# Attention: the blocks of v loaded straight from memory on two queues, in place of a spread on GpSimd

## The chip, the cores and the metric

The kernel runs on one core of one Trainium2 chip. A core has TensorE (matrix multiply, PE in the profile, with its weight loads as PEld), VectorE (DVE), ScalarE (ACT), GpSimd (POOL) and SyncE (SP), and 16 DMA engines that move data between device memory and the on-chip memories. The metric is the device time of one execution, in microseconds (us), and the median of several executions is what counts. All data is 32-bit floating point.

## The reference, cut to what matters

The network has two parts: a gated convolution through a Fourier transform, and an attention over heads. The change is in the second alone. For every one of 8 x 56 x 56 tokens (25088 in all) it has 8 heads of 16 values.

```python
q, k, v = xs @ Wq.T, xs @ Wk.T, 2 * (xs @ Wv.T)         # each to (b, n, HEADS, DIM_HEAD)
q, k, v_h = _l2norm(q), _l2norm(k), _l2norm(v)
attn_head = softmax(einsum('bnhd,bngd->bnhg', v_h, v_h))  # 8 x 8 for each token
q = einsum('bnhg,bngd->bnhd', attn_head, q)
k = einsum('bnhg,bngd->bnhd', attn_head, k)
attn = softmax(einsum('bnhd,bnhe->bnde', k, q))           # 16 x 16 for each token
out = einsum('bnhd,bnde->bnhe', v, attn)
```

The output is then projected, and the residual is added.

## The kernel before

`build` runs its stages one after the other: weights, input projection, taps of the filter, convolution, output projection, `attend`, `project_heads`. Only `attend` changes.

`attend` works in 112 units of 224 tokens (NU), two units to a block of 448 tokens (NB = 56 blocks). A unit has 14 groups (GU) of 16 tokens. Each engine has its own program with the order written out by hand, and semaphores tie the programs together.

A block goes through a first half: TensorE projects it to q, k and v (`project`, L1180), ScalarE squares and copies (`copy_in`) and takes roots (`root`), VectorE normalizes (`normalize_q`, `normalize_kv`; the normalized v is `st_v`, L1360), GpSimd copies the norms (`copy_norm`, L1146), and ScalarE's queue stores v and the q/k rows to device memory (`store_heads`, L1283 and L1284). It is read back in another layout, one partition for each pair of token and head or of token and value. This first half runs 8 units ahead (AU) of the second.

The second half goes unit by unit. On TensorE a round i consists of `scores(i)`, `logits(i-1)`, `project(i+8)`, `mix(i)` and `outputs(i-1)`. Both `scores` (v times v, L1190) and `outputs` (L1226) read the tile `v_blocks`: 128 partitions by 14 groups by 2 rows by 64 columns, in which partition 64a + q + 4d holds value d of the token of slot (a, q), in the 8 columns of that slot, and zeros in the other 56. There are three such tiles in a ring (RING = 3).

Before the change these tiles are made in two steps. SyncE loads a block's v densely (`load_v`, L1113: 8 transfers for each block, each to every fourth of 64 partitions, four ring tiles `v_dense`); then GpSimd multiplies each dense tile, broadcast over 8 slots, by a mask `slot_of_8` (`spread_v`, L1154, once for each unit, 128 x 1792 elements). `spread_v(u)` waits until `outputs` of unit u-3 is done. After `spread_v(i+1)` GpSimd goes on to `spread_k(i)` (L1139), which makes `k_blocks` for `logits(i)` from what ScalarE's `leave_mix(i)` (L1304, L1305) wrote.

VectorE's round i is `mask(i)` (L1367, makes `e_blocks` for `mix(i)`), `divide(i-1)` (L1384 to L1390, makes `p_norm` for `outputs(i-1)`), `weigh(i)`, one half of a block's normalizing (`normalize_q` where i is even, `normalize_kv` where it is odd), `leave(i-1)` (L1395, frees the q/k rows) and `squares`. ScalarE's is `exp_s(i)`, on even i `store_heads`, then `exp_l(i-1)` (L1296), `copy_in`, `leave_mix(i)`, on even i `root` (L1277), and `copy_in` again.

The functions that the diff touches, and what calls them:

Of the kernel before, what the change touches and what calls it, by code (L numbers as in the profile page):

```python
# [13 lines left out]
HEADS, HD = 8, 16  # L14
# [53 lines left out]
def load_weights(nc, t, k):  # L68


    with ExitStack() as ctx:
# [25 lines left out]
                     (k.fwd_w[:], t.c_fwd_w), (k.tap_p[:], t.c_tap_p), (k.tap_q[:], t.c_tap_q),  # L97
                     (k.inv_w[:], t.c_inv_w), (k.dc[:], t.c_dc), (k.inv_h[:], t.c_inv_h), (k.same4[:], t.c_same4), (k.same8[:], t.c_same8), (k.slot8[:], t.c_slot8),
                     (k.rpe_in[0:2, :], t.L0_conv_rpe_in_w.rearrange("o i -> i o")),
# [926 lines left out]
def attend(nc, t, k):  # L1026
# [17 lines left out]
    RING = 3  # L1044
    NV = 4
    LOOPED = (NU - AU) // RING
    MC = (GU + 3) * HD
    MW = GU // 2 * QKM
    with ExitStack() as ctx:
# [14 lines left out]
        vb = [sb(f"v_blocks{m}", [128, GU, 2, 64]) for m in range(RING)]  # L1064
        vd = [sb(f"v_dense{m}", [128, 4 * GU, HEADS]) for m in range(NV)]
        qk = [sb(f"qk_rows{m}", [128, GU + 1, QKW]) for m in range(RING)]
# [13 lines left out]
        st_stored = [sem(f"st_stored{m}") for m in range(2)]  # L1080
        v_loaded = [sem(f"v_dense_loaded{m}") for m in range(NV)]
        qk_loaded = [sem(f"qk_loaded{m}") for m in range(RING)]
        cleared, vb_r, k_r, qkv_ps, qkv_read = sem("cleared"), sem("v_blocks_ready"), sem("k_blocks_ready"), sem("qkv_ps"), sem("qkv_read")
        nsq_r, nsc_r, nrm_r, rn_r, st_r, vn_r = (sem(n) for n in ("nsq_ready", "nsq_clamped", "nrm_ready", "rnorm_ready", "st_ready", "v_norm_ready"))
# [6 lines left out]
        def unit(i):  # L1091
            return not isinstance(i, int) or 0 <= i < NU

        @block.sync
        def _(sp):
            def load_xn(w):
                if w >= NU:
                    return
                if w >= RING:
                    sp.wait_ge(qkv_ps, 2 * (w - RING) + 2)  # L1100
                b, c = w // UPI, w % UPI
                sp.dma_start(xn[w % RING][:], t.XN[b, :, c * UT:(c + 1) * UT]).then_inc(xn_loaded[w % RING], 16)

            def load_v(n):
                if n >= NB:
                    return
                if n >= NV:
                    sp.wait_ge(vb_r, 2 * (n - NV) + 2)
                sp.wait_ge(st_stored[n % 2], 32 * (n // 2 + 1))
                v = t.VT[n * 2 * UT:(n + 1) * 2 * UT].rearrange("(x a q) (d h) -> a q d x h", q=4, a=2, h=HEADS)  # L1110
                for a in range(2):
                    for q in range(4):
                        sp.dma_start(vd[n % NV][64 * a + q:64 * a + 64:4], v[a, q]).then_inc(v_loaded[n % NV], 16)  # L1113

            def load_qk(u):
                m, n = u % RING, u // 2
                if u < RING:
                    sp.wait_ge(cleared, 1)
                else:
                    sp.wait_ge(o_r, u - RING + 1)  # L1120
                sp.wait_ge(st_stored[n % 2], 32 * (n // 2 + 1))
                sp.dma_start(qk[m][:, 0:GU, :], t.QK[u * UT:(u + 1) * UT].rearrange("(g n) h x -> (n h) g x", n=16)).then_inc(qk_loaded[m], 16)

            for w in range(AU + 1):
                load_xn(w)
            load_v(0)
            for u in range(NU):
                load_qk(u)
                load_xn(u + AU + 1)
                if u % 2 == 0:  # L1130
                    load_v(u // 2 + 1)

        @block.gpsimd
        def _(pool):
            def spread_k(i):
                pool.wait_ge(km_r, i + 1)
                if i:
                    pool.wait_ge(l_ps, i)
                pool.tensor_tensor(kb[:], bcast(km[i % 2][:], 3, 4), bcast(bcast(k.same4[:], 1, HD), 1, GU), ALU.mult).then_inc(k_r, 1)  # L1139

            def copy_norm(n):
                a = n % 2
                pool.wait_ge(nrm_r, n + 1)
                if n >= 2:
                    pool.wait_ge(st_stored[a], 32 * (n // 2))
                pool.tensor_copy(st_qk[a][:, :, :, QKM], nrm[a][:, :, 16:24]).then_inc(vn_r, 1)  # L1146

            def spread_v(u):
                n, g0 = u // 2, u % 2 * 2 * GU
                if u % 2 == 0:  # L1150
                    pool.wait_ge(v_loaded[n % NV], 128 * (n // NV + 1))
                if u >= RING:
                    pool.wait_ge(o_ps, u - RING + 1)
                pool.tensor_tensor(vb[u % RING][:].rearrange("p g r (m h) -> p (g r) m h", h=HEADS),  # L1154
                                   bcast(vd[n % NV][:, g0:g0 + 2 * GU], 2, 8),
                                   bcast(k.slot8[:].rearrange("p (m h) -> p m h", h=HEADS), 1, 2 * GU), ALU.mult).then_inc(vb_r, 1)

            for m in range(RING):
                last = pool.memset(qk[m][:, GU:, :], 0.0)
            last.then_inc(cleared, 1)  # L1160
            for n in range(AHEAD - 1):
                copy_norm(n)
            spread_v(0)
            spread_v(1)
            for i in range(NU):
                spread_k(i)
                if i + 2 < NU:
                    spread_v(i + 2)
                if i % 2 == 0 and i // 2 + AHEAD - 1 < NB:
                    copy_norm(i // 2 + AHEAD - 1)  # L1170

        @block.tensor
        def _(pe):
# [30 lines left out]

            def mix(i, m, loads):
                pe.wait_ge(qk_loaded[m], loads * 16)
                pe.wait_ge(e_r, i + 1)
                if not isinstance(i, int) or i:
                    pe.wait_ge(l_exp, i)
                pe.sem_inc(mix_seen, 1)  # L1210
                for g in range(GU):
                    for a in range(2):
                        rows = slice(64 * a, 64 * a + 64)
                        half, at = 64 * (a ^ g % 2), MC + g // 2 * QKM
                        last = pe.matmul(ps_l[half:half + 64, g % 2, at:min(at + 64, 512)], eb[rows, g, :],  # L1215
                                         strided(qk[m][rows], g * QKW, [[1, min(64, 512 - at)]]), start=True, stop=True)
                last.then_inc(m_ps, 1)
# [12 lines left out]
            def round_of(c, j):  # L1230
                i = c * RING + j
                if unit(i):
                    scores(i, j)
                if unit(i - 1):
# [4 lines left out]
                if unit(i):  # L1239
                    mix(i, j, c + 1)  # L1240
                if unit(i - 1):
                    outputs(i - 1, (j - 1) % RING)


            for _ in range(80):
                pe.sem_inc(aligned, 1)
# [12 lines left out]
        def _(act):  # L1259
# [233 lines left out]
def build(nc, t):  # L1493
    scratch(nc, t)
    with ExitStack() as ctx:
# [9 lines left out]
        k.dc = sb("zero_freq", [1, NFFT])  # L1505
        k.same4, k.same8, k.slot8 = sb("same_of_4", [128, 4]), sb("same_of_8", [128, 64]), sb("slot_of_8", [128, 64])
        k.fwd_h, k.fwd_w = sb("fwd_h", [64 + SIDE, 2 * NF]), sb("fwd_w", [120, 2, NFFT])
# [13 lines left out]
def tables():  # L1521
# [31 lines left out]
    c["c_same8"] = np.tile(np.kron(np.eye(8), np.ones((HEADS, HEADS))), (2, 1))  # L1553
    p = np.arange(128)
    c["c_slot8"] = np.repeat((4 * (p // 64) + p % 4)[:, None] == np.arange(8), HEADS, axis=1)
    q, p = np.meshgrid(np.arange(NFFT), np.arange(TAPS), indexing="ij")
# [29 lines left out]
```

## Time and profile before

| | us |
|---|---|
| median of 3 executions | 3363.04 (3359.36 to 3363.75) |
| the profiled execution, its own time | 3362.75 |
| its span, first to last instruction | 3360.9 |
| PE busy | 2928.1 (87%) |
| DVE busy | 2212.1 (66%) |
| ACT busy | 1265.6 (38%) |
| POOL busy | 1068.1 (32%) |

The span is 1.9 us shorter than the execution's time, and the execution is 0.3 us off the median. Busy times are sums over all stages; `attend` is the stretch from about 2021 to 3238 us. Time stamps in the rows are microseconds from the start of the span. TensorE's clock can be granted in part: a granted clock of 1.00 is the full 2.4 GHz, and a mean below it says that for part of the stretch the lower level was granted.

### The profile page before, as it was taken

The page shows a single profiled execution, that of the slowest core. Times are in us where ns is not written, and L with a number is a line of the kernel's source. Part 1 is how long each engine was busy: PE and PEld are TensorE (multiplying, and loading weights), DVE is VectorE, ACT ScalarE, POOL GpSimd, SP SyncE. Part 2 cuts the span into 40 slices and gives each one's busy share as a digit, 9 for nine tenths or more (in the row PEclk, how much of TensorE's full clock was granted, in tenths as well). Part 3 has the DMA queues.
Part 4 walks back from the last instruction along what each step waited for, and adds up shares of the span by engine and source line. Part 5 has one row for each costly group of instructions (what it writes and reads, how often), then busy time and mean ns, then how long its engine had stood idle before and what let it go on. Part 6 is the DMA issues. An engine that isn't in the chain of part 4 may idle for free. (4 is left out here: it accounts for less than half of the span.)

```text
span 3360.9 us, 145079 instructions
## 1 busy us (share of the span) xinstructions
PE 2928.1 (87%) x62769; PEld 2176.7 (65%) x62769; DVE 2212.1 (66%) x3276; ACT 1265.6 (38%) x2841; POOL 1068.1 (32%) x582
## 2 busy tenths in 40 slices
PE   6676989999999999999998984788888888888779
PEld 5554369766666666666664443677676776777679
DVE  4452542566666666666665764888888888888733
ACT  3454452422222222222223443444454444444300
POOL 0000030022222222222221222566666665666520
PEclk7778889999999999999999996999999999999999
DMA  6877000021111111111115974455444454554446
GB/s 141 220 223 205 2 1 1 12 46 45 45 44 44 45 45 45 44 45 45 44 44 221 411 295 85 74 85 81 80 80 80 79 82 80 81 80 80 74 114 206
DMA packets 1025871, 315.46 MB, mean 94 GB/s; under 512 B 865409, under 2 KB 1011390, under 8 KB 1021630
## 3 DMA queue, kind: packets, MB, share of 16 engines
q1 hardware_dynamic: 703890, 182.66, 24.9%
q10 hardware_dynamic: 321836, 130.92, 14.6%
q8 instruction: 85, 1.39, 0.2%
q14 instruction: 60, 0.49, 0.0%
HBM read 157.70 MB, written 155.75 MB: 93 GB/s over the span
## 5 line engine op out<-in xcount | busy, mean ns | idle before, releaser
L845 DVE TENSOR_TENSOR terms<-spec,ps_z 112x456 f32<-112x456 f32 x1024 | 575.5, 624 | 403.8 <-PE ps_z L728 403.8
L826 POOL TENSOR_TENSOR prod<-terms 112x456 f32<-112x456 f32 x256 | 297.7, 1163 | 998.9 <-DVE terms L845 998.9
L738 PEld LDWEIGHTS ps_q<-inv_w,prod 112*57 112x57 f32 x16384 | 450.9, 133 | 174.7 <-issue 172.2
L1154 POOL TENSOR_TENSOR v_blocks<-v_dense,slot_of 128x1792 f32<-128x1792 f32 x112 | 461.2, 4118 | 88.7 <-PE ps_o L1226 80.3
L738 PE MATMUL ps_q<-inv_w,prod 112*57 112x56 f32 x16384 | 484.4, 217 | 1.3 <-DVE prod L851 1.3
L728 PE MATMUL ps_z<-x_half,fwd_w 120*112 120x456 f32 x1024 | 458.4, 570 | 0.0
L783 ACT ACTIVATE q_half<-ps_q 121x448 f32<-121x448 f32 x255 | 139.2, 546 | 827.1 <-PE ps_y L746 827.1
L1226 PE MATMUL ps_o<-p_norm,v_blocks 128*64 128x64 f32 x6272 | 272.1, 262 | 49.0 <-DVE p_norm L1390 46.7
L1139 POOL TENSOR_TENSOR k_blocks<-k_mixed,same_of 128x896 f32<-128x896 f32 x112 | 188.3, 1681 | 380.8 <-ACT k_mixed L1305 380.8
L1226 PEld LDWEIGHTS ps_o<-p_norm,v_blocks 128*64 128x64 f32 x6272 | 255.1, 174 | 62.9 <-DVE p_norm L1390 60.2
L1215 PE MATMUL ps_l<-qk_rows,e_blocks 64*64 64x64 f32 (+1 forms) x6272 | 124.2, 230 | 169.5 <-DVE e_blocks L1367 137.1
L1215 PEld LDWEIGHTS ps_l<-qk_rows,e_blocks 64*64 64x64 f32 x6272 | 113.1, 143 | 232.3 <-issue 232.3
L728 PEld LDWEIGHTS ps_z<-x_half,fwd_w 120*112 120x112 f32 x1024 | 160.4, 176 | 121.9 <-issue 106.1
L1367 DVE TENSOR_TENSOR e_blocks<-s_exp,same_of 128x896 f32<-128x896 f32 x112 | 190.3, 1699 | 71.3 <-ACT s_exp L1290 71.3
L1360 DVE TENSOR_TENSOR st_v<-qkv,rnorm 112x512 f32<-112x512 f32 x56 | 231.3, 4131 | 0.0
L1190 PE MATMUL ps_s<-v_blocks 128*64 128x64 f32 x6272 | 210.8, 227 | 5.2 <-POOL v_blocks L1154 5.1
L1201 PE MATMUL ps_l<-q_mixed,k_blocks 32*64 32x64 f32 x12544 | 210.7, 219 | 5.1 <-issue 5.1
L1180 PE MATMUL ps_qkv<-weights,xn_in 128*112 128x384 f32 x448 | 179.2, 524 | 36.3 <-issue 24.2
L1190 PEld LDWEIGHTS ps_s<-v_blocks 128*64 128x64 f32 x6272 | 201.7, 143 | 7.0 <-POOL v_blocks L1154 6.3
L1201 PEld LDWEIGHTS ps_l<-q_mixed,k_blocks 32*64 32x64 f32 x12544 | 194.2, 133 | 13.7 <-issue 6.1
L720 PEld LDWEIGHTS ps_x<-fwd_h,v_in 56*56 56x56 f32 x8192 | 130.0, 128 | 91.9 <-issue 91.8
L1290 ACT ACTIVATE s_exp<-ps_s 128x896 f32<-128x896 f32 x112 | 102.8, 918 | 210.3 <-PE ps_s L1190 210.2
(135 smaller groups left out, 4628.3 us busy)
## 6 DMA issues: line engine op xcount, KB each, us to landing
qk_heads<-st_qk ACTq DMA_DIRECT2D x56, 476.0 KB, 4.8
qk_rows<-qk_heads SPq DMA_DIRECT2D x112, 238.0 KB, 4.2
conv_in<-v_sb ACTq DMA_DIRECT2D x112, 224.0 KB, 3.3
v_in<-conv_in SPq DMA_DIRECT2D x512, 49.0 KB
conv_out<-y_sb ACTq DMA_DIRECT2D x512, 49.0 KB
y<-conv_out SPq DMA_DIRECT2D x8, 1792.0 KB, 13.4
x_in<-in_x SPq DMA_DIRECT2D x8, 1568.0 KB, 9.5
shortcut<-short ACTq DMA_DIRECT2D x8, 1568.0 KB, 6.2
```

The costliest lines, as they stand in the source:

```text
L728: last = pe.matmul(ps_z[b % 2][x][0:NFFT, 0:PC], k.fwd_w[:, x, :], x_half[b % 2][:].rearrange("p r x -> p (r x)"), start=True, stop=True)
L738: last = pe.matmul(ps_q[64 * ri:64 * ri + NF, c * SIDE:(c + 1) * SIDE], prod[b % 2][:, x, c * NF:(c + 1) * NF], k.inv_w[:, x, ri * SIDE:(r ...
L826: pool.tensor_tensor(prod[b % 2][:, 1, :], terms[b % 2][:, 2, :], terms[b % 2][:, 3, :], ALU.add).then_inc(prod_i_r, 1)
L845: last = dve.tensor_tensor(terms[b % 2][:, x, :], k.spec[0:NFFT, s, bass.ds(c * CC, CC), :].rearrange("p c f -> p (c f)"), ps_z[b % 2][z][ ...
L1139: pool.tensor_tensor(kb[:], bcast(km[i % 2][:], 3, 4), bcast(bcast(k.same4[:], 1, HD), 1, GU), ALU.mult).then_inc(k_r, 1)
L1154: pool.tensor_tensor(vb[u % RING][:].rearrange("p g r (m h) -> p (g r) m h", h=HEADS), bcast(vd[n % NV][:, g0:g0 + 2 * GU], 2, 8), bcast(k ...
L1190: last = pe.matmul(to, vb[m][:, g, a, :], vb[m][:, g, a, :], start=True, stop=True)
L1201: last = pe.matmul(ps_l[half:half + 64, s // 2, g * HD:g * HD + 64], kb[rows, g].rearrange("p d m -> p (d m)"), qm[rows, g:g + 4, :], star ...
L1215: last = pe.matmul(ps_l[half:half + 64, g % 2, at:min(at + 64, 512)], eb[rows, g, :], strided(qk[m][rows], g * QKW, [[1, min(64, 512 - at) ...
L1226: last = pe.matmul(ps_o[64 * r:64 * r + 64, g * HD:g * HD + 64], vb[m][:, g, r, :], pn[:, a, g:g + 4, :], start=True, stop=True)
L1360: dve.tensor_tensor(st_v[a][:].rearrange("p j (d h) -> p j d h", h=HEADS), qkv[a][:, :, 2 * CH:].rearrange("p j (d h) -> p j d h", h=HEADS ...
L1367: dve.tensor_tensor(eb[:], ex[:], bcast(k.same8[:], 1, GU), ALU.mult).then_inc(e_r, 1)
```

## The change

GpSimd's multiply, the dense tiles and the mask constant go. The three `v_blocks` tiles are cleared once, and the 8 columns of each slot are filled by transfers from device memory, unit by unit: eight for each unit, of 448 runs of 32 bytes each (before: eight for each block, of 896 such runs). Four of them (a = 0) are issued by SyncE, the other four (a = 1) by GpSimd, on its own queue. Both wait until `outputs` of unit u-3 is done. `scores` now waits for the v transfers of both queues, and for the load of the q/k rows too, which counts on the same semaphore as SyncE's v transfers. On GpSimd the four transfers of unit i+1 are issued ahead of `spread_k(i)`. On ScalarE `store_heads` is moved from behind `exp_s(i)` to behind `leave_mix(i)`.

```diff
-            def load_v(n):
-                if n >= NV:
-                    sp.wait_ge(vb_r, 2 * (n - NV) + 2)
-                sp.wait_ge(st_stored[n % 2], 32 * (n // 2 + 1))
-                v = t.VT[n * 2 * UT:(n + 1) * 2 * UT].rearrange("(x a q) (d h) -> a q d x h", q=4, a=2, h=HEADS)
-                for a in range(2):
-                    for q in range(4):
-                        sp.dma_start(vd[n % NV][64 * a + q:64 * a + 64:4], v[a, q]).then_inc(v_loaded[n % NV], 16)
...
+        def v_block(u, a, q):
+            at8 = (4 * a + q) * HEADS
+            return vb[u % RING][64 * a + q:64 * a + 64:4, :, :, at8:at8 + HEADS]
+
+        def v_rows(u):
+            return t.VT[u * UT:(u + 1) * UT].rearrange("(g r a q) (d h) -> a q d g r h", q=4, r=2, a=2, h=HEADS)
...
+            def turn(u):
+                at = slice(u * UT, (u + 1) * UT)
                 m, n = u % RING, u // 2
                 if u < RING:
-                    sp.wait_ge(cleared, 1)
+                    sp.wait_ge(cleared, m + 1)
                 else:
+                    sp.wait_ge(o_ps, u - RING + 1)
+                sp.wait_ge(st_stored[n % 2], 32 * (n // 2 + 1))
+                for q in range(4):
+                    sp.dma_start(v_block(u, 0, q), v_rows(u)[0, q]).then_inc(in_loaded[m], 16)
+                if u >= RING:
                     sp.wait_ge(o_r, u - RING + 1)
-                sp.dma_start(qk[m][:, 0:GU, :], t.QK[u * UT:(u + 1) * UT].rearrange("(g n) h x -> (n h) g x", n=16)).then_inc(qk_loaded[m], 16)
+                sp.dma_start(qk[m][:, 0:GU, :], t.QK[at].rearrange("(g n) h x -> (n h) g x", n=16)).then_inc(in_loaded[m], 16)
...
             for u in range(NU):
-                load_qk(u)
+                turn(u)
                 load_xn(u + AU + 1)
-                if u % 2 == 0:
-                    load_v(u // 2 + 1)
...
-            def spread_v(u):
...
-                pool.tensor_tensor(vb[u % RING][:].rearrange("p g r (m h) -> p (g r) m h", h=HEADS),
-                                   bcast(vd[n % NV][:, g0:g0 + 2 * GU], 2, 8),
-                                   bcast(k.slot8[:].rearrange("p (m h) -> p m h", h=HEADS), 1, 2 * GU), ALU.mult).then_inc(vb_r, 1)
+            def turn_half(u):
+                m, n = u % RING, u // 2
+                if u < RING:
+                    pool.wait_ge(cleared, m + 1)
+                else:
+                    pool.wait_ge(o_ps, u - RING + 1)
+                pool.wait_ge(st_stored[n % 2], 32 * (n // 2 + 1))
+                for q in range(4):
+                    pool.dma_start(v_block(u, 1, q), v_rows(u)[1, q]).then_inc(half_loaded[m], 16)
 
             for m in range(RING):
-                last = pool.memset(qk[m][:, GU:, :], 0.0)
-            last.then_inc(cleared, 1)
+                pool.memset(qk[m][:, GU:, :], 0.0)
+                pool.memset(vb[m][:], 0.0).then_inc(cleared, 1)
             for n in range(AHEAD - 1):
                 copy_norm(n)
-            spread_v(0)
-            spread_v(1)
+            for u in range(RING):
+                turn_half(u)
             for i in range(NU):
+                if i >= RING - 1 and unit(i + 1):
+                    turn_half(i + 1)
                 spread_k(i)
-                if i + 2 < NU:
-                    spread_v(i + 2)
                 if i % 2 == 0 and i // 2 + AHEAD - 1 < NB:
                     copy_norm(i // 2 + AHEAD - 1)
...
-            def scores(i, m):
-                pe.wait_ge(vb_r, i + 1)
+            def scores(i, m, loads):
+                pe.wait_ge(in_loaded[m], loads * 80)
+                pe.wait_ge(half_loaded[m], loads * 64)
...
-            def mix(i, m, loads):
-                pe.wait_ge(qk_loaded[m], loads * 16)
+            def mix(i, m):
...
                 if unit(i):
                     exp_s(i)
-                if i % 2 == 0 and i and i // 2 + AHEAD - 2 < NB:
-                    store_heads(i // 2 + AHEAD - 2)
                 if unit(i - 1):
                     exp_l(i - 1)
                 if unit(i + AU):
                     copy_in(2 * (i + AU))
                 if unit(i):
                     leave_mix(i)
+                if i % 2 == 0 and i and i // 2 + AHEAD - 2 < NB:
+                    store_heads(i // 2 + AHEAD - 2)
                 if i % 2 == 0 and i // 2 + AHEAD - 1 < NB:
                     root(i // 2 + AHEAD - 1)
```

## Rows read from the trace of the kernel before

**Rows 1.** The windows view of a long and a short round (stretch first, then its length).

```profile
2508.15:2520.04 11.89, 9.16 (x290) 7.99 (x286) 10.42 (x13) 5.27 (x13) 5.99 (x3) 0.86 0.46 96
2520.04:2528.70 8.66, 7.78 (x291) 6.63 (x289) 7.57 (x10) 4.97 (x11) 6.68 (x3) 1.00 0.53 59
```

**Rows 2.** The view of waits, 2110 to 3150 us (total us, times, longest).

```profile
ACT p_exp L1296 <- DVE st_v L1360: 151.6, 47, 3.4
...
PE ps_l L1215 <- DVE e_blocks L1367: 121.6, 49, 2.7
```

**Rows 3.** Two lines of code, whole span: durations in ns (min/median/max).

```profile
L1360 DVE TENSOR_TENSOR st_v<-qkv,rnorm x56: 677/4469/4482, 2048.4 to 3174.7; 112x512 f32<-112x512 f32 x56
...
L1367 DVE TENSOR_TENSOR e_blocks<-s_exp,same_of x112: 1070/1087/2991, 2078.0 to 3223.4; 128x896 f32<-128x896 f32 x112
```

**Rows 4.** The timeline of one short round (start, duration in us).

```profile
2520.10 1.80 PE L1190 MATMUL ps_s<-v_blocks 128*64 128x64 f32 x56
...
2520.58 0.57 DVE L1395 TENSOR_TENSOR oT<-ps_o,qk_rows 128x224 f32<-128x224 f32 x1
2520.98 0.93 DVE L1335 TENSOR_REDUCE nsq<-sq 112x48 f32<-112x768 f32 x1
...
2521.83 1.86 PE L1201 MATMUL ps_l<-q_mixed,k_blocks 32*64 32x64 f32 x112
...
2522.90 2.57 DVE L1367 TENSOR_TENSOR e_blocks<-s_exp,same_of 128x896 f32<-128x896 f32 x1 [0.99 <-ACT s_exp L1290]
2523.62 1.54 PE L1180 MATMUL ps_qkv<-weights,xn_in 128*112 128x384 f32 x4
...
2525.57 1.03 PE L1215 MATMUL ps_l<-qk_rows,e_blocks 64*64 64x64 f32 x56 [0.40 <-issue]
...
2527.07 1.85 PE L1226 MATMUL ps_o<-p_norm,v_blocks 128*64 128x64 f32 x56 [0.48 <-DVE p_norm L1390]
2527.16 1.68 POOL L1139 TENSOR_TENSOR k_blocks<-k_mixed,same_of 128x896 f32<-128x896 f32 x1 [1.59 <-ACT k_mixed L1305]
```

**Rows 5.** The timeline of the long round behind it.

```profile
2529.02 4.21 POOL L1154 TENSOR_TENSOR v_blocks<-v_dense,slot_of 128x1792 f32<-128x1792 f32 x1 [0.18 <-PE ps_o L1226]
2529.31 4.47 DVE L1360 TENSOR_TENSOR st_v<-qkv,rnorm 112x512 f32<-112x512 f32 x1
...
2533.81 0.31 ACTq L1283 DMA_DIRECT2D v_heads<-st_v  x1
...
2534.15 0.51 ACTq L1284 DMA_DIRECT2D qk_heads<-st_qk  x1
...
2536.36 1.33 PE L1215 MATMUL ps_l<-qk_rows,e_blocks 64*64 64x64 f32 x56 [2.54 <-DVE e_blocks L1367]
...
2537.87 2.95 PE L1226 MATMUL ps_o<-p_norm,v_blocks 128*64 128x64 f32 x56 [0.17 <-DVE p_norm L1390]
...
2539.48 0.29 ACT L1277 ACTIVATE nrm<-nsq_c 112x96 f32<-112x96 f32 x1
2539.79 0.75 DVE L1351 RECIPROCAL rnorm<-nrm 112x96 f32<-112x96 f32 x1 [1.15 <-ACT nrm L1277]
```

**Rows 6.** The timeline of SyncE's queue: a block's eight transfers of v.

```profile
2501.93 6.12 SPq L1113 DMA_DIRECT2D v_dense<-v_heads  x8
```

**Rows 7.** The page's DMA issues (KB each, median us from issue to landing).

```profile
qk_rows<-qk_heads SPq DMA_DIRECT2D x112, 238.0 KB, 4.2
...
v_dense<-v_heads SPq DMA_DIRECT2D x448, 28.0 KB, 3.9
```

**Rows 8.** The timeline at the start of the stage.

```profile
2041.51 0.24 POOL L1146 COPY st_qk<-nrm 112x32 f32<-112x32 f32 x1 [20.30 <-ACT nrm L1277]
...
2056.68 0.24 POOL L1146 COPY st_qk<-nrm 112x32 f32<-112x32 f32 x1 [9.61 <-ACT nrm L1277]
...
2069.23 3.25 PE L1190 MATMUL ps_s<-v_blocks 128*64 128x64 f32 x56 [5.13 <-POOL v_blocks L1154]
```

**Rows 9.** The windows view from the start of round 104 to the stage's end.

```profile
3153.60:3238.00 84.40, 62.17 (x2415) 59.08 (x2410) 49.89 (x69) 18.53 (x36) 42.67 (x16) 0.90 0.31 47
```

More of the change, by code:

```diff
@@ L97, in load_weights @@
                      (k.fwd_w[:], t.c_fwd_w), (k.tap_p[:], t.c_tap_p), (k.tap_q[:], t.c_tap_q),
-                     (k.inv_w[:], t.c_inv_w), (k.dc[:], t.c_dc), (k.inv_h[:], t.c_inv_h), (k.same4[:], t.c_same4), (k.same8[:], t.c_same8), (k.slot8[:], t.c_slot8),
+                     (k.inv_w[:], t.c_inv_w), (k.dc[:], t.c_dc), (k.inv_h[:], t.c_inv_h), (k.same4[:], t.c_same4), (k.same8[:], t.c_same8),
                      (k.rpe_in[0:2, :], t.L0_conv_rpe_in_w.rearrange("o i -> i o")),
@@ L1044, in attend @@
     RING = 3
-    NV = 4
     LOOPED = (NU - AU) // RING
@@ L1064, in attend @@
         vb = [sb(f"v_blocks{m}", [128, GU, 2, 64]) for m in range(RING)]
-        vd = [sb(f"v_dense{m}", [128, 4 * GU, HEADS]) for m in range(NV)]
         qk = [sb(f"qk_rows{m}", [128, GU + 1, QKW]) for m in range(RING)]
@@ L1080, in attend @@
         st_stored = [sem(f"st_stored{m}") for m in range(2)]
-        v_loaded = [sem(f"v_dense_loaded{m}") for m in range(NV)]
-        qk_loaded = [sem(f"qk_loaded{m}") for m in range(RING)]
-        cleared, vb_r, k_r, qkv_ps, qkv_read = sem("cleared"), sem("v_blocks_ready"), sem("k_blocks_ready"), sem("qkv_ps"), sem("qkv_read")
+        half_loaded = [sem(f"half_loaded{m}") for m in range(RING)]
+        in_loaded = [sem(f"in_loaded{m}") for m in range(RING)]
+        cleared, k_r, qkv_ps, qkv_read = sem("cleared"), sem("k_blocks_ready"), sem("qkv_ps"), sem("qkv_read")
         nsq_r, nsc_r, nrm_r, rn_r, st_r, vn_r = (sem(n) for n in ("nsq_ready", "nsq_clamped", "nrm_ready", "rnorm_ready", "st_ready", "v_norm_ready"))
@@ L1146, in copy_norm @@
                 pool.tensor_copy(st_qk[a][:, :, :, QKM], nrm[a][:, :, 16:24]).then_inc(vn_r, 1)
-            def spread_v(u):
[L1149 to L1152, printed above, removed]
+            def turn_half(u):
[3 more added lines that the diff above has]
+                else:
                     pool.wait_ge(o_ps, u - RING + 1)
-                pool.tensor_tensor(vb[u % RING][:].rearrange("p g r (m h) -> p (g r) m h", h=HEADS),
-                                   bcast(vd[n % NV][:, g0:g0 + 2 * GU], 2, 8),
-                                   bcast(k.slot8[:].rearrange("p (m h) -> p m h", h=HEADS), 1, 2 * GU), ALU.mult).then_inc(vb_r, 1)
+                pool.wait_ge(st_stored[n % 2], 32 * (n // 2 + 1))
+                for q in range(4):
+                    pool.dma_start(v_block(u, 1, q), v_rows(u)[1, q]).then_inc(half_loaded[m], 16)
             for m in range(RING):
-                last = pool.memset(qk[m][:, GU:, :], 0.0)
-            last.then_inc(cleared, 1)
+                pool.memset(qk[m][:, GU:, :], 0.0)
+                pool.memset(vb[m][:], 0.0).then_inc(cleared, 1)
             for n in range(AHEAD - 1):
                 copy_norm(n)
-            spread_v(0)
-            spread_v(1)
+            for u in range(RING):
+                turn_half(u)
             for i in range(NU):
+                if i >= RING - 1 and unit(i + 1):
+                    turn_half(i + 1)
                 spread_k(i)
-                if i + 2 < NU:
-                    spread_v(i + 2)
                 if i % 2 == 0 and i // 2 + AHEAD - 1 < NB:
@@ L1232, in round_of @@
                 if unit(i):
-                    scores(i, j)
+                    scores(i, j, c + 1)
                 if unit(i - 1):
@@ L1239, in round_of @@
                 if unit(i):
-                    mix(i, j, c + 1)
+                    mix(i, j)
                 if unit(i - 1):
                     outputs(i - 1, (j - 1) % RING)
-            for _ in range(80):
+            for _ in range(81):
                 pe.sem_inc(aligned, 1)
@@ L1505, in build @@
         k.dc = sb("zero_freq", [1, NFFT])
-        k.same4, k.same8, k.slot8 = sb("same_of_4", [128, 4]), sb("same_of_8", [128, 64]), sb("slot_of_8", [128, 64])
+        k.same4, k.same8 = sb("same_of_4", [128, 4]), sb("same_of_8", [128, 64])
         k.fwd_h, k.fwd_w = sb("fwd_h", [64 + SIDE, 2 * NF]), sb("fwd_w", [120, 2, NFFT])
@@ L1553, in tables @@
     c["c_same8"] = np.tile(np.kron(np.eye(8), np.ones((HEADS, HEADS))), (2, 1))
-    p = np.arange(128)
-    c["c_slot8"] = np.repeat((4 * (p // 64) + p % 4)[:, None] == np.arange(8), HEADS, axis=1)
     q, p = np.meshgrid(np.arange(NFFT), np.arange(TAPS), indexing="ij")
```

5 lines of the change are left out of this document (removed).

## The prediction

> **What bounds the kernel now.** I read the windows view over the whole span first. Of the stages only the attention changes, and there TensorE is not full. I then cut the attention into rounds by the starts of `scores`. Rounds alternate: 11.9 us where i is even, 8.7 where it is odd [rows 1], so a calm pair lasts 20.6. In the long one the clock granted to TensorE is 0.86 on average, in the short one 1.00. From the first `scores` at 2069.2 to that of round 104 at 3153.6 [rows 8, 9] there are 104 rounds in 1084.4 us, 10.43 each, so an average pair (20.86) is 0.30 longer than a calm one.
>
> TensorE's own work, read off the short round, is 1.80 + 1.86 + 1.54 + 1.03 + 1.85 = 8.08 us [rows 4]. The short round adds two waits, 0.40 before `mix` and 0.48 before `outputs`. The long one has 3.8 us more than the work, and the timeline says why [rows 5]: `st_v` on VectorE starts at 2529.31, just behind GpSimd's `spread_v` at 2529.02, and takes 4.47 us where it can take 0.68 [rows 3]. Next late is ScalarE, whose `store_heads` waits for `st_v` and holds `exp_l` behind it (151.6 us in 47 waits), then `e_blocks`, for which TensorE waits 2.5 us (121.6 us in 49) [rows 2]. After that wait `outputs` takes 2.95 instead of 1.85 [rows 4, 5], in the round whose clock is lower. In the short round it is `mask` that runs beside `spread_v`, and takes 2.57 instead of 1.09 [rows 3, 4]. So the bound is TensorE, plus the time by which GpSimd's multiply holds VectorE up.
>
> **The change, part by part.** *`spread_v` goes:* 4.2 us of GpSimd's time for each of 112 units [rows 5]. In steady state nobody waits for it, so it is worth what it gives back on VectorE: 3.8 us for each long `st_v`, 1.5 for each short round's `mask`. With `mask` done in 1.09 it ends at 2523.99, before `project` is through at 2525.16, so the 0.40 goes; `divide` starts 1.5 earlier, and the 0.48 goes. In the long round, `leave`, `squares` and `mask` come about 3.8 us earlier, `e_blocks` is ready in time, there is no idle stretch behind which the clock falls, and `outputs` is 1.85 again. Both rounds would be 8.08, 16.16 a pair. That is the floor.
>
> *`store_heads` moved behind `leave_mix`:* its gain is counted already (`exp_l` waits for no `st_v`). Its price is on what now stands behind it: `root`, whose result VectorE's `rnorm` already waits 1.15 us for [rows 5]. The two issues take 0.85, start of the first to end of the second [rows 5]. `nrm` is done 3.4 us after `mix` starts [rows 5], and `mix` starts at 5.2 in a round without waits; so `nrm` comes at 8.6 + 0.85 = 9.45. Behind it VectorE has `rnorm` (0.75), the q rows (0.68, the shape of `st_v`), `leave` (0.57) and `squares` (0.93) [rows 3 to 5]: 12.4, which is 4.3 into the next round. `mask` takes 1.1, and `outputs` can start 1.5 after `mask` is done, as in the long round [rows 5]: at 6.9, where TensorE would be ready at 6.2. That is a wait of 0.7 a pair.
>
> *The transfers.* A unit has 8 x 448 runs, as many as before, so the DMA engines' work is unchanged. Eight transfers of 896 runs were issued in 6.12 us [rows 6], 0.77 each; that rate I take for the engines' own, so 3.06 us for a unit's v. SyncE's four of half the runs then cost 1.5 to 2 us, ahead of the q/k load and `xn`; its turn of about 4 us fits in a round of 8. The q/k load is issued behind `leave`, which after an even round ends 3.4 us into the next; it lands 4.2 later [rows 7], at 7.6 or somewhat after. Before, `mix` waited for it; now `scores`, 5 us sooner.
>
> The Trainium skill speaks against a gain from the second queue: "DMA: Bandwidth & Descriptors", section "Rules for kernel authors", says that transfers spread over SyncE, ScalarE and GpSimd share the same 16 engines and interleave, and that splitting by partition halves is no help. By that rule a unit's v takes the same 3.06 us, and the sum below is as it stands; if each queue had its own bandwidth, v would be there 1.5 us sooner and a pair would take about 1 us less, 52 us in all.
>
> *GpSimd's four issues.* No transfer of the trace before is issued by GpSimd, so c, the time that one takes there, is unknown. From below: ScalarE's issue of `v_heads`, also 448 runs, took 0.31 [rows 5]. From above: if GpSimd handles each run as it handles a column of a tensor, `spread_v` gives 4.2 / 1792 = 2.3 ns [rows 5], 1.05 us for 448 runs, or 2.1 if it goes over source and target in turn; on top a fixed part, 0.24 by the shortest copy [rows 8]. So 0.3 to 2.35. I take 1.2: the issue is most like GpSimd's own work, gone once over the runs.
>
> For the same path the skill's "DMA: Bandwidth & Descriptors", section "Specifications", gives about 1 us to the first byte, against 0.6 for SyncE's; with c = 1.0 as an estimate from that page, the sum would be some 30 us lower.
>
> With c = 1.2, count from the start of a round. GpSimd may start unit i+1's four when `outputs(i-2)` is done, which is this moment, and they must land before the next round. The `spread_k` of the round before started 1.59 after `mix` and took 1.68 [rows 4]: it ended at 5.2 + 3.27 = 8.5, which is 0.4 into this one. The four start there, the last at 0.4 + 3.6 = 4.0, landing 3.9 later [rows 7] at 7.9: hidden. After an even round `copy_norm` is in between; it waits for `nrm`, at 9.45, and takes 0.24, so the four start at 1.6 and have landed at 9.1. `scores` waits till then, and this covers the 0.7 at `outputs` in the same round and a q/k load up to 9. A pair is 8.1 + 9.1 = 17.2, and with the 0.30 of irregularity carried over 17.5, 8.75 a round. `spread_k(i)` behind the four (4.8 us) could start at 5.2 to 6.4, before its input at 6.8: not late.
>
> *Start and end.* The clearing of three tiles is hidden, since GpSimd is idle for 20.3 us before 2041.5 [rows 8]; at the 2.3 ns a column of above it is 12 us, and without the cover that would be its price. The first four go out behind the copy at 2056.7 and land by 2057 + 3.6 + 3.9 = 2064.5, so `scores` starts some 4 us sooner than at 2069.2, where it waited 5.1 for GpSimd [rows 8]. The last eight rounds take 10.5 us each with the end of the stage [rows 9] and have no `project`; there the loads (8 us) and not TensorE (6.5) set the pace, and I take 1 us off each.
>
> **The sum.** 4 + 104 x (10.43 - 8.75) + 8 = 4 + 175 + 8 = 187 off. From the profiled execution's 3362.75 (span 3360.9 and 1.9 around it; 0.3 under the median) that gives 3176.
>
> **The rivals.**
> *A, the forecast:* c near 1.2, and GpSimd's chain adds about 1 us a pair. 3176, own range 3120 to 3240.
> *B, GpSimd becomes the bound (slower).* Its round is 4c + 1.68 + 0.12 (half a copy) + about 0.1. It reaches the 10.43 of before at c = 2.13, inside my bounds. At c = 3 it is 13.9, which is 3.5 x 112 = 390 us more: 3750. For it speaks that 448 runs of 32 bytes a transfer are many for software, and that the upper bound lies past the turning point; against it that once over the runs is the likelier end. TensorE's `logits` would then wait for GpSimd's `spread_k`.
> *C, the loads come late, but not that late.* With c of 1.5 to 2, or landings a microsecond later, the round is set by issue and landing: at c = 1.8 GpSimd's round is 4c + 1.9 = 9.1, and 3c + 3.9 = 9.3 from a start that is at times late; I take 9.4. That is 112 x 1.03 = 115 off: 3248, range 3220 to 3350. VectorE could cause it as well: if its instructions held GpSimd up at each issue as `spread_v` held up `st_v`, by some 0.6 us (half of `mask`), c = 1.2 would be 1.8. The skill's page "SBUF — State Buffer", section "Who interferes with whom", has a lock that starves GpSimd's transfers, but only beside VectorE's copies, casts and tensor-scalar operations; here that is one short `clamp` a pair, so by the page nothing is added.
> *D, full relief:* c under 0.8 and prompt landings; rounds near the floor, 8.2 with the irregularity: 4 + 104 x 2.2 + 12 = 245 off, 3118.
>
> **Chances.** A 0.48, C 0.20, D 0.08, B 0.22, and 0.02 for a place between C and B where nothing changes. What this measurement can tell from no change is about 0.2%, 7 us. Faster 0.76, same 0.02, slower 0.22. The range goes from below D's case to just past no change, 3100 to 3380; it leaves out nearly all of B, 0.2.
>
> **What would show it.** `st_v` at 0.68 and `mask` at 1.09 throughout; no wait of ScalarE for `st_v`; a granted clock near 1.00 in both rounds; `scores` waiting about 1 us for a transfer in every second round; GpSimd issuing transfers at 1.2 us each; `rnorm` waiting about 2 us for `nrm`. It would be wrong if c is above 2 (B), if transfers of GpSimd's queue land much later than the 3.9 of SyncE's, or if `st_v` stays long although `spread_v` is gone.

## The result and the profile after

The changed kernel takes 3128.88 us (median of 4 executions, 3125.82 to 3134.22) against 3363.39 before: the ratio is 0.9306 with a 95% interval of 0.929 to 0.9322, 234.5 us less. The prediction was 3176, 187 less. The profiled execution took 3134.22 us, with a span of 3132.4. An execution counts as slow when it is over 1.5% above the fastest of its kernel, and of all those below only the slowest of the kernel with all transfers on SyncE is one.

The windows view of the 104 rounds with `project`, first of the kernel before, then of the changed one. Behind the stretch and its length stand the busy times of PE, PEld, DVE, ACT and POOL, then the granted clock, the DMA engines' share and GB/s. The third line is the changed kernel's last eight rounds, to the end of the last matmul; its counterpart is [rows 9], which runs 1.45 us further, to 3238.00, where the last matmul ends at 3236.55.

```profile
2069.23:3153.61 1084.38, 881.48 (x29369) 760.94 (x29371) 940.53 (x1089) 533.15 (x1196) 655.77 (x260) 0.92 0.50 80
```

```profile
2069.02:2925.99 856.97, 809.22 (x29367) 692.06 (x29369) 676.33 (x1090) 529.45 (x1196) 437.64 (x568) 1.00 0.67 101
2925.99:3007.56 81.57, 63.53 (x2415) 59.80 (x2411) 39.10 (x68) 18.53 (x36) 30.99 (x38) 0.90 0.39 53
```

The stretch is 227.4 us shorter: 8.24 us a round in place of 10.43. TensorE runs the same instructions, and the 227.4 divide into 155.1 of idle time (202.9 to 47.8) and 72.3 of busy time, because the clock granted is 1.00 in place of 0.92. VectorE does the same 1090 instructions in 264 us less; about 193 of these are `st_v` (52 times, 4.40 us on average before and 0.68 after) and 64 are `mask` (104 times, 1.71 and 1.09). The last eight rounds gain 1.4 us only (82.94 to 81.57, each to the end of the last matmul); TensorE's clock is 0.90 there as before.

The windows view of two rounds after, an odd one and the even one behind it, against [rows 1]:

```profile
2476.16:2484.78 8.62, 7.83 (x292) 6.68 (x290) 6.95 (x11) 6.79 (x16) 4.93 (x7) 1.00 0.75 124
2484.78:2492.54 7.76, 7.76 (x290) 6.64 (x287) 6.06 (x11) 3.51 (x8) 3.72 (x6) 1.00 0.65 83
```

The timeline over the even round from 2484.78 (against [rows 5]) and the start of the odd one:

```profile
2484.78 1.80 PE L1187 MATMUL ps_s<-v_blocks 128*64 128x64 f32 x56
2485.00 2.65 SPq L1118 DMA_DIRECT2D v_blocks<-v_heads  x4
2485.28 2.43 POOL L1152 DMA_DIRECT2D v_blocks<-v_heads  x4 [0.37 <-PE ps_o L1222]
2485.39 0.68 DVE L1356 TENSOR_TENSOR st_v<-qkv,rnorm 112x512 f32<-112x512 f32 x1
...
2490.93 0.31 ACTq L1279 DMA_DIRECT2D v_heads<-st_v  x1
...
2493.19 0.28 ACT L1273 ACTIVATE nrm<-nsq_c 112x96 f32<-112x96 f32 x1
...
2493.51 0.75 DVE L1347 RECIPROCAL rnorm<-nrm 112x96 f32<-112x96 f32 x1 [1.73 <-ACT nrm L1273]
...
2494.01 2.44 POOL L1152 DMA_DIRECT2D v_blocks<-v_heads  x4 [0.23 <-issue]
...
2497.84 1.03 PE L1211 MATMUL ps_l<-qk_rows,e_blocks 64*64 64x64 f32 x56 [0.18 <-DVE e_blocks L1363]
```

`st_v` takes 0.68, GpSimd's four issues 2.43 together, and `nrm`, behind the stores on ScalarE, is what VectorE now waits for. The whole-span views of single lines (ns, min/median/max) say the same for all instructions, against [rows 3]; the third is the price that no row of before had:

```profile
L1356 DVE TENSOR_TENSOR st_v<-qkv,rnorm x56: 676/678/684, 2052.3 to 2946.1; 112x512 f32<-112x512 f32 x56
...
L1363 DVE TENSOR_TENSOR e_blocks<-s_exp,same_of x112: 1083/1092/1094, 2075.9 to 2995.0; 128x896 f32<-128x896 f32 x112
...
L1152 POOL DMA_DIRECT2D v_blocks<-v_heads x448: 608/608/785, 2061.2 to 2985.8; - x150
```

And the waits, 2110 to 2950 us, against [rows 2]. The wait of ScalarE for `st_v` is gone; TensorE's largest are 20.8 for `p_norm` and 14.9 for `e_blocks`, and for a load it waited once:

```profile
DVE rnorm L1347 <- ACT nrm L1273: 89.1, 51, 2.7
...
PE ps_o L1222 <- DVE p_norm L1386: 20.8, 48, 0.5
...
PE ps_l L1211 <- DVE e_blocks L1363: 14.9, 48, 0.6
...
PE ps_s L1187 <- DMA qk_rows<-qk_heads: 1.3, 1, 1.3
```

### The profile page after: what moved, and what is told of

Same layout as the page of the kernel before. It is cut to its first block and busy times, and to the rows that moved or that the text cites. A ratio compares the mean times of both kernels' runs of the same rounds, so it can differ in the third digit from the quotient of the medians.

```text
span 3132.4 us, 145347 instructions
## 1 busy us (share of the span) xinstructions
PE 2862.5 (91%) x62769; PEld 2113.4 (67%) x62769; DVE 1933.0 (62%) x3276; ACT 1262.5 (40%) x2841; POOL 843.7 (27%) x921
## 3 DMA queue, kind: packets, MB, share of 16 engines
q0 software_dynamic: 14336, 6.45, 3.7%
## 5 line engine op out<-in xcount | busy, mean ns | idle before, releaser
L1152 POOL DMA_DIRECT2D v_blocks<-v_heads x448 | 272.7, 615 | 41.7 <-PE ps_o L1222 23.5
L1222 PE MATMUL ps_o<-p_norm,v_blocks 128*64 128x64 f32 x6272 | 213.4, 227 | 26.5 <-DVE p_norm L1386 23.6
L1222 PEld LDWEIGHTS ps_o<-p_norm,v_blocks 128*64 128x64 f32 x6272 | 197.4, 141 | 36.0 <-DVE p_norm L1386 29.8
L1211 PEld LDWEIGHTS ps_l<-qk_rows,e_blocks 64*64 64x64 f32 x6272 | 106.3, 136 | 92.4 <-issue 92.4
L720 PE MATMUL ps_x<-fwd_h,v_in 56*56 56x57 f32 x8192 | 164.0, 218 | 4.6 <-DMA v_in<-conv_in 3.8
L851 DVE TENSOR_TENSOR prod<-terms 112x456 f32<-112x456 f32 x256 | 161.9, 633 | 8.8
L457 POOL TENSOR_TENSOR features<-features,last_rinv 111x2048 f32<-111x2048 f32 x7 | 25.2, 3608 | 478.7 <-DVE last_rinv L636 478.7
```

The costliest lines, as they stand in the source:

```text
L720: last = pe.matmul(ps_x[64 * ri:64 * ri + SIDE, r, c * NF:(c + 1) * NF], v_in[b % 2][rows, c * SIDE:(c + 1) * SIDE], k.fwd_h[rows, ri * NF ...
L851: dve.tensor_tensor(prod[b % 2][:, 0, :], terms[b % 2][:, 0, :], terms[b % 2][:, 1, :], ALU.subtract).then_inc(prod_r, 1)
L1152: pool.dma_start(v_block(u, 1, q), v_rows(u)[1, q]).then_inc(half_loaded[m], 16)
L1222: last = pe.matmul(ps_o[64 * r:64 * r + 64, g * HD:g * HD + 64], vb[m][:, g, r, :], pn[:, a, g:g + 4, :], start=True, stop=True)
```

## The experiments

All times are medians, of two to five executions, and every ratio is against the kernel before, run beside it on the same chip (3362 to 3364 us).

**One part alone: `store_heads` moved, the rest as before.**

```diff
 # the kernel before, ScalarE
                 if unit(i):
                     exp_s(i)
-                if i % 2 == 0 and i and i // 2 + AHEAD - 2 < NB:
-                    store_heads(i // 2 + AHEAD - 2)
...
                     leave_mix(i)
+                if i % 2 == 0 and i and i // 2 + AHEAD - 2 < NB:
+                    store_heads(i // 2 + AHEAD - 2)
```

> The kernel before with one part of the change alone: store_heads stands behind leave_mix; spread_v and the dense loads stay. Theory V (VectorE is held up by GpSimd's reads in spread_v): exp_l no longer waits for st_v, but st_v still takes 4.5 us, and e_blocks of the long round hangs on VectorE's own order (st_v, leave, squares, mask), so mix still waits about 2.5 us in every second round; 3350 to 3370, within 0.4% of before. Rival S (ScalarE's order was the cause, the way that v takes is neutral): the wait of 3.2 us per pair goes with this part, 3200 or less.

Measured: 3392.48, ratio 1.0085 (1.0061 to 1.011). Neither theory has it right: it is slower by 29 us. The large part of the gain does not come from the order, so the rival S falls. The timeline of this kernel shows the price:

```profile
2499.25 3.90 DVE L1345 TENSOR_TENSOR st_qk<-qkv,rnorm 112x512 f32<-112x512 f32 x1
...
2505.48 1.03 PE L1215 MATMUL ps_l<-qk_rows,e_blocks 64*64 64x64 f32 x56 [2.15 <-issue]
```

With the stores ahead of `root`, `nrm` and so the q rows come later (`rnorm` waits 1.69 in place of 1.15), and here they start behind `spread_v` (2498.60, 3.99 us). They take 3.90, where they take 0.69 when they start ahead of it. That short round is then 10.4 in place of 8.7 and has nearly the wait before `mix` of the long one. From 2110 to 2950 us this happens in 20 of 40 pairs, in the kernel before in 4 of 40. A delay of some half a microsecond costs 1.7 in such a pair because it moves an instruction under GpSimd's multiply.

**The other part alone: v by transfers, `store_heads` at its old place.**

```diff
 # the changed kernel, ScalarE
                     exp_s(i)
+                if i % 2 == 0 and i and i // 2 + AHEAD - 2 < NB:
+                    store_heads(i // 2 + AHEAD - 2)
...
                     leave_mix(i)
-                if i % 2 == 0 and i and i // 2 + AHEAD - 2 < NB:
-                    store_heads(i // 2 + AHEAD - 2)
```

> The changed kernel with store_heads put back to where it was before, behind exp_s. Theory V: st_v is done 1.3 us into the round, before exp_s is, so nothing waits for it; the two issues fill time in which ScalarE waits for logits, root comes 0.6 to 0.85 us sooner in every even round, rnorm waits about 1 us in place of 1.7, and some of the 0.8 us that mix and outputs wait in a pair goes: 3090 to 3115, faster than the changed kernel. Rival S: exp_l is held up again and 3200 or more.

Measured: 3145.94, ratio 0.9351 (0.9333 to 0.937). The transfers in place of `spread_v` bring nearly all of the change by themselves, but my expectation that this would beat the changed kernel was wrong: it is some 0.5% slower (17 us), and the intervals don't overlap. The waits of this kernel, 2110 to 2950 us:

```profile
DVE rnorm L1347 <- ACT nrm L1273: 58.3, 51, 1.1
...
PE ps_s L1187 <- DMA qk_rows<-qk_heads: 55.3, 49, 2.0
```

The first half came as expected: `rnorm` waits 1.1 instead of 1.7, and TensorE's waits for `p_norm` and `e_blocks` are gone. In their place `scores` waits for the q/k load in every second round. The stores are issued at 1.9 us into the round, in the middle of the unit's loads:

```profile
2486.15 2.55 SPq L1118 DMA_DIRECT2D v_blocks<-v_heads  x4
...
2487.84 0.31 ACTq L1279 DMA_DIRECT2D v_heads<-st_v  x1
2488.18 0.70 ACTq L1280 DMA_DIRECT2D qk_heads<-st_qk  x1
2488.75 0.64 SPq L1121 DMA_DIRECT2D qk_rows<-qk_heads  x1
...
2495.09 1.85 PE L1187 MATMUL ps_s<-v_blocks 128*64 128x64 f32 x56 [1.35 <-DMA qk_rows<-qk_heads]
```

The median from issue to landing of the q/k load is 5.0 us here (up to 6.9), against 4.2 before [rows 7]. In this round it releases `scores` 6.3 us after its issue (2488.75 to 2495.09). In the changed kernel it is issued as late in the round, at 2487.69, and `scores` starts without a wait 4.9 us later, at 2492.54.

**A multiply of the size of `spread_v` put back, for nobody.** In the changed kernel, on GpSimd behind the four issues (its input tile is cleared at the start, which the cut leaves out):

```diff
                 if i >= RING - 1 and unit(i + 1):
                     turn_half(i + 1)
+                    pool.wait_ge(idle_done, i - RING + 1)
+                    pool.tensor_tensor(idle_out[:], bcast(idle_in[:, 0:2 * GU], 2, 8),
+                                       bcast(idle_in[:, 2 * GU:2 * GU + 8], 1, 2 * GU), ALU.mult).then_inc(idle_done, 1)
```

> The changed kernel, and on GpSimd, behind the four issues of every round, one multiply of the size of spread_v (128 x 1792, both inputs read, tiles of its own that nobody waits for). Theory V: it lies from about 2.8 to 7.0 us of each round, over mask; mask takes 3 to 5 us, mix waits for e_blocks, rounds of 10.5 to 12: 3350 to 3550. Rival G (what counted was GpSimd's time, not its reads): GpSimd is busy 2.5 + 4.2 + 1.7 = 8.4 us a round, a little over the 8.2 of now: 3130 to 3170, mask at 1.1.

Measured: 3551.67, ratio 1.0561 (1.0537 to 1.0585). `mask` takes 3.73 on average, against 1.09:

```profile
2512.73 5.04 DVE L1371 TENSOR_TENSOR e_blocks<-s_exp,same_of 128x896 f32<-128x896 f32 x1 [0.85 <-ACT s_exp L1294]
2512.85 3.96 POOL L1170 TENSOR_TENSOR idle_out<-idle_in 128x1792 f32<-128x1792 f32 x1
```

It is slower even than the kernel before, and just above my range. From 2110 to 2950 us the multiply meets `mask` in 48 of 70 rounds, and `mask` then takes 4.5 to 5.3 us. In the other 22 it meets VectorE's `clamp` just ahead of `mask`, which takes 4.4 us in place of 0.21, and `mask` is as late for it. So both rounds of a pair are long.

**The same time on GpSimd without reads.** The same place, three memsets in place of the multiply:

```diff
+                    for x, rows in enumerate((2 * GU, 2 * GU, 18)):
+                        pool.wait_ge(idle_done, 3 * (i - RING + 1) + x)
+                        pool.memset(idle_out[:, 0:rows], 0.0).then_inc(idle_done, 1)
```

> The same place, but three memsets of about the same total length (1792, 1792 and 1152 columns, 1.6 us for 1792 in the changed kernel's start), which read nothing. Theory V: VectorE's instructions keep their durations (mask 1.09, st_v 0.68), GpSimd is busy 8.4 us a round: 3130 to 3180. A rival by which any instruction of GpSimd holds VectorE up: as with the multiply, 3350 or more.

Measured: 3179.08, ratio 0.9453 (0.9431 to 0.9476). The memsets take 4.4 us a round, more than the multiply. `mask` stays at 1.10, but that alone shows nothing, since the memsets reach over it in only 4 of 97 rounds (2110 to 2950 us). What shows it is `st_v`: it starts while the memsets run and takes 0.69, where beside `spread_v` it took 4.47 [rows 3, 5]. So it is not GpSimd's time that holds VectorE's two-input instructions up; the multiply and the memsets both write, and what the multiply does besides is read. What the 50 us over the changed kernel are is seen in the timeline; GpSimd is now full, and `logits` waits for `spread_k` (72.5 us in 93 waits), as my rival B had it:

```profile
2500.32 1.86 PE L1206 MATMUL ps_l<-q_mixed,k_blocks 32*64 32x64 f32 x112 [0.95 <-POOL k_blocks L1137]
...
2508.79 1.86 PE L1206 MATMUL ps_l<-q_mixed,k_blocks 32*64 32x64 f32 x112 [0.62 <-POOL k_blocks L1137]
...
2511.66 4.38 POOL L1171 MEMSET idle_out<- 128x1792 f32 x3
...
2514.58 0.69 DVE L1364 TENSOR_TENSOR st_v<-qkv,rnorm 112x512 f32<-112x512 f32 x1
```

**All eight transfers on SyncE**, `turn` with a loop over a = 0, 1, and GpSimd's `turn_half` gone. The counts for which `scores` waits follow, here and in the next two.

```diff
-                for q in range(4):
-                    sp.dma_start(v_block(u, 0, q), v_rows(u)[0, q]).then_inc(in_loaded[m], 16)
+                for a in range(2):
+                    for q in range(4):
+                        sp.dma_start(v_block(u, a, q), v_rows(u)[a, q]).then_inc(in_loaded[m], 16)
```

> The changed kernel with all eight transfers of a unit issued by SyncE. Theory V (the gain is VectorE's freedom; the second queue carries no bandwidth of its own): the DMA engines' work is the same, but SyncE's turn becomes 8 x 0.66 + 0.6 + 1.6 = 7.5 us of a round of 8.2, so the q/k load lands at 10 or later and scores waits for it: 3140 to 3220, still far below before. Theory Q (the second queue is what makes it fast): 3250 or more. If the queue did not matter at all, 3130.

Measured: 3212.36 (3195.36 to 3246.38), ratio 0.9583 (0.953 to 0.9637). It scatters more than the other kernels; without its slowest execution the median is 3198.67.

**All eight on GpSimd**, the same edit in `turn_half`, and SyncE left with the q/k load.

> The changed kernel with all eight issued by GpSimd at the 0.615 us that the changed kernel shows. GpSimd's round is 8 x 0.615 + 1.68 + 0.1 = 6.7 us, under 8.2; the last is issued at 4.3 (5.9 in odd rounds) and lands 3 to 4 later. If GpSimd's issues cost 0.615 whatever else, and land as SyncE's do: 3130 to 3170. If the transfers of GpSimd's queue are the costly ones for the DMA engines: 3180 or more.

Measured: 3168.44, ratio 0.9417 (0.9402 to 0.9431). SyncE's queue in the one kernel and TensorE's wait there (2110 to 2950 us), then a wait of GpSimd's kernel:

```profile
2507.19 5.75 SPq L1119 DMA_DIRECT2D v_blocks<-v_heads  x8
2512.98 0.61 SPq L1122 DMA_DIRECT2D qk_rows<-qk_heads  x1
2513.63 1.45 SPq L1107 DMA_DIRECT2D xn_in<-x_mid_normed  x1
```

```profile
PE ps_s L1183 <- DMA qk_rows<-qk_heads: 69.6, 83, 2.3
```

```profile
PE ps_s L1186 <- DMA v_blocks<-v_heads: 10.9, 16, 1.4
```

SyncE's turn is 7.8 us of a round of 8.8, and the q/k load goes out 5.8 us after the first of the eight, where in the changed kernel it goes out 2.7 after the first of four. GpSimd issues eight in 4.93, and `scores` waits 30.7 us in all, 10.9 for v and 19.8 with no releaser in the profile. Both are faster than before by more than the second queue is worth, which is 84 us against SyncE alone (70 without its slowest execution) and 40 against GpSimd alone. On SyncE it is worth issue time. The DMA engines are not full in any of the three: their mean share from 2110 to 2900 us is 0.68 with four on each queue, 0.58 with eight on SyncE and 0.68 with eight on GpSimd. So these runs show no bandwidth of its own, and don't rule it out either.

**GpSimd's transfers cut in two**, for the price of an issue.

```diff
                 for q in range(4):
-                    pool.dma_start(v_block(u, 1, q), v_rows(u)[1, q]).then_inc(half_loaded[m], 16)
+                    for g in range(0, GU, GU // 2):
+                        pool.dma_start(v_block(u, 1, q)[:, g:g + GU // 2], v_rows(u)[1, q][:, g:g + GU // 2]).then_inc(half_loaded[m], 16)
```

> The changed kernel with each of GpSimd's four transfers cut in two (8 of 224 runs in place of 4 of 448; the work moved is the same). It separates the two parts of the term c: if c is nearly all per run, as the prediction had it (1.05 of 1.2), an issue of 224 runs takes 0.35 or less and the time stays at 3129; if it is fixed, an issue stays near 0.6, eight take 4.8 us, and the time is 3130 to 3160.

Measured: 3132.89, ratio 0.9313 (0.9291 to 0.9336), the same as the changed kernel. Its line, in ns:

```profile
L1153 POOL DMA_DIRECT2D v_blocks<-v_heads x896: 550/550/724, 2051.2 to 2981.1; - x180
```

608 for 448 runs and 550 for 224 give 0.26 ns a run and 0.49 us that did not change with the runs. c is nearly all fixed.

**The stores at the same point of the round, one round later.**

```diff
 # the changed kernel, ScalarE, behind leave_mix
-                if i % 2 == 0 and i and i // 2 + AHEAD - 2 < NB:
+                if i % 2 and i > 2 and i // 2 + AHEAD - 2 < NB:
                     store_heads(i // 2 + AHEAD - 2)
```

> The changed kernel with store_heads at the same point of the round, behind leave_mix, but in odd rounds in place of even ones, one round later. There no root stands behind it and ScalarE waits 2.6 us for scores. If the two issues ahead of root cost what the prediction said (0.6 us on ScalarE, 0.7 to 0.8 of TensorE's waits a pair) and the stores' transfers stay clear of the unit's loads: 3085 to 3110. If the wait that goes comes back as a wait for the loads, as with the stores at their old place: 3125 to 3150.

Measured: 3101.07, ratio 0.9219 (0.9206 to 0.9231): faster than the changed kernel by 0.9%, 28 us. Waits, 2110 to 2950 us:

```profile
DVE rnorm L1347 <- ACT nrm L1273: 57.3, 50, 1.1
...
PE ps_o L1222 <- DVE p_norm L1386: 10.3, 33, 0.6
```

`rnorm` waits as little as with the stores at their old place, and the waits of `scores` for a load are down to one of 0.3 us. TensorE's waits for `p_norm` and `e_blocks` fall from 35.7 to 11.1 us in these 840 us, and that is the gain.

**The stores at the old place, and `mix` in place of `scores` waiting for the q/k load.**

```diff
-                sp.dma_start(qk[m][:, 0:GU, :], t.QK[at].rearrange("(g n) h x -> (n h) g x", n=16)).then_inc(in_loaded[m], 16)
+                sp.dma_start(qk[m][:, 0:GU, :], t.QK[at].rearrange("(g n) h x -> (n h) g x", n=16)).then_inc(qk_loaded[m], 16)
...
-                pe.wait_ge(in_loaded[m], loads * 80)
+                pe.wait_ge(in_loaded[m], loads * 64)
...
             def mix(i, m, loads):
+                pe.wait_ge(qk_loaded[m], loads * 16)
```

> The changed kernel with store_heads back behind exp_s (as in the run that moved it back) and the q/k load on a semaphore of its own, for which mix waits and not scores. In that run scores waited up to 1.8 us in every second round, by the trace for the q/k load. If that is the wait, it is gone here, since mix comes 5 us later: rounds of 7.8, 3085 to 3110. If v's own transfers are as late (the stores' transfers push all loads back), scores still waits 0.5 to 1.5 us: 3125 to 3150.

Measured: 3101.42, ratio 0.9225 (0.9209 to 0.924). The 44 us against the run with the stores there and the shared semaphore are the wait for the q/k load, which still lands 5.3 us after its issue; v's own transfers are in time (1.3 us of waits in 840).

**Both.** The odd rounds and the semaphore apart.

> store_heads in odd rounds, behind leave_mix, and the q/k load on its own semaphore. In the run with the odd rounds alone scores waited for a load once in 840 us, so the semaphore has nothing left to take away: 3095 to 3107, the same as that run. If loads that arrive just in time still cost something: 3085 or less.

Measured: 3100.61, ratio 0.9224 (0.9207 to 0.9242): nothing more. The changed kernel pays for stores ahead of `root`, its variant with the stores at the old place pays for stores over the loads, and each of the two edits arrives at a kernel that pays for neither.

## Why the prediction was right, and where its sizes were off

**What bounds it and what `spread_v` costs: right, and shown.** `st_v` is at 0.68 and `mask` at 1.09 throughout, `exp_l` no longer waits, both rounds have clock 1.00. The multiply put back for nobody restores the loss, and memsets of the same length don't. What the prediction did not see is that the same effect is left in the changed kernel: `st_qk` of the k rows takes 1.91 us in place of 0.69 once a pair, beside `spread_k`. It costs no time there: in the even round behind it (2484.78) TensorE is busy throughout.

**The floor of 8.08: too high.** I added durations, and neighbouring groups of matmuls overlap at their ends. The short round before gives it from start to start: 8.65 (2520.10 to 2528.75) less the two waits, 7.77. After, a round without waits takes 7.63 to 7.77, 7.69 on average (18 of them from 2400 on). This is the largest error: 2 x 0.38 = 0.76 us a pair, 40 us over 52 pairs, since it stood in both rounds of the sum.

**c, the issue on GpSimd: 0.61 in place of 1.2.** I priced it as GpSimd's column work, 2.3 ns a run; it is 0.26 ns a run and 0.49 fixed. The Trainium skill's "DMA: Bandwidth & Descriptors", section "Specifications", would have pointed nearer (about 1 us to the first byte), though what is paid on GpSimd is less than that. With c = 0.61 the last of the four goes out 1.47 + 3 x 0.61 = 3.3 us into the round after an even one (predicted 4.0 to 5.2), nothing waits for it, and the 0.3 a pair by which it exceeded the wait at `outputs` (9.1 against 8.08 + 0.7) is not there, some 17 us. That is all that a smaller c can bring by the prediction's own terms, so its "some 30 us lower" for c = 1.0 was a slip. The sign "`scores` waiting about 1 us in every second round" did not come. The start at 1.6 into that round was right (1.47).

**`store_heads` behind `leave_mix`: the price right, the benefit missed.** A wait of 0.7 a pair was predicted; it is 0.70 on average (35.7 us in 51 pairs), at `mix` and `outputs` together, and `rnorm` waits 1.73 where I had 2. But I took its gain as counted in `exp_l`. Once `spread_v` is gone, nothing waits for `st_v`; what the new place brings is that the stores' transfers no longer lie over the unit's loads. Without the move the kernel is some 0.5% slower.

**The q/k load in `scores`: the risk was seen (landing at 7.6 or after), and it is real at the stores' old place, hidden at the new one.**

**The second queue.** The Trainium skill's "DMA: Bandwidth & Descriptors", section "Rules for kernel authors", leaves it no bandwidth but the sequencer's issue time, and of this the prediction took the first half alone. No run here shows a bandwidth of its own. The issue time counts, since 8 x 0.72 us of issues on SyncE delay what is behind them. My reading of 6.12 us for eight transfers as the DMA engines' rate was wrong: SyncE's issue of half the runs took as long (median 624 ns), so its four take 2.6, not 1.5 to 2.

**Start and end.** In this execution the stage begins 3.9 us later than in that of before (first copy of norms at 2045.44 against 2041.51); 3.7 of it were there already in the convolution (GpSimd's first `prod` at 660.6 against 656.9), so it is not of the change. The first `scores` is at 2069.02: 4.1 sooner by the stage's own clock, as predicted. The end gave 1.4 and not 8. There TensorE's waits for `e_blocks` are gone (12.8 us in 7 waits), and `scores` waits for no load, against the prediction; but TensorE now sits idle 10.9 us ahead of and inside its groups of matmuls where the profile names no releaser (1.6 before), and the clock is 0.90 as it was. What these are stays open.

Added up, for the profiled executions: 4.1 - 3.9 + 227.4 + 1.4 - 0.5 (what stands behind the stage is that much longer) = 228.5, which is what the spans differ by; predicted 187. Of the 53 us by which the stretch was underrated (175 against 227.4) the floor is 40, c 17, and the irregularity 4 (I carried over 0.30 a pair, and 0.22 is there: 16.48 on average, 16.26 in a calm stretch); against them stand 9, since the long round exceeds the short one by 0.87 and not by 0.7. The floor and c erred towards too little gain, the end towards too much. Of the rivals, D came nearest in its condition (c under 0.8) and in its time (3118, 11 us off; A's 3176 is 47 off), A in its mechanism (odd rounds longer by what `nrm` is late). B was wrong in the size of c; the wait it named does appear once GpSimd is filled to 8.7 us a round. C's late loads appear with the stores at their old place.

## What to carry to other kernels

Before an instruction is moved or added on an engine, look at what it comes to lie beside on the others: here 4 us of reads on GpSimd cost VectorE 3.8 in one round and 1.5 in the next, with no wait of VectorE for GpSimd in the view of waits, and a half-microsecond shift in the order cost 29 us. Such a hold shows where one instruction's shortest and median durations differ. Take the floor of a pipelined engine from start to start, less the waits, and not from a sum of durations. When loads become just-in-time, place stores where they delay neither a load that is waited for nor a needed instruction behind them, or let each consumer wait for its own load alone; either led to some 28 us less here.

## What the runs showed of the hardware

An issue of a DMA on GpSimd costs 0.49 us and 0.26 ns a run (448 and 224 runs of 32 bytes). SyncE's costs 0.62 for 448 and 0.66 for 896 (medians). GpSimd's queue moved its runs in fewer packets: 14336 for 448 transfers of 448 runs, 14 runs to a packet. SyncE's queue has 200704 packets less than before, one for each of the 200704 runs that it no longer moves.

`st_v`, which has two inputs, takes 4.47 us beside `spread_v`, 0.69 beside memsets and 0.68 beside GpSimd's issues. `q_mixed` also has two, but one is `ps_l`, which the matmuls wrote; it takes 0.39 beside `spread_k` as it does beside memsets. `clamp`, a tensor-scalar operation, takes 0.21 us in the kernel before and 4.4 beside the multiply put back. In the run with memsets it takes 1.26, but beside `spread_k`, not the memsets. In the changed kernel it takes 0.39 beside GpSimd's issues, and beside those of half the runs 0.21 again, so what in an issue holds it is not shown. The Trainium skill's page "SBUF — State Buffer", section "Who interferes with whom", says that a VectorE instruction with two inputs in SBUF contends with a GpSimd instruction that reads and not with one that only writes, and that tensor-scalar operations can contend as well; these durations agree. The part of it that would have starved GpSimd's transfers did not matter: the issues stayed at 0.608 to 0.785.

With TensorE's short idle stretches gone, the granted clock over 857 us is 1.00 where it was 0.92, and 72 of the 227 us are this.
